# Delta rule attention on one core: key products in a spare bank, projections in another step, another order of masks and copies

## The chip, the core and the metric

The kernel runs on one core of a Trainium2 chip. The metric is the time of one launch on the device in microseconds (us), lower is better. Engines are named as in the profile: PE is TensorE's matmuls and PEld its weight loads, DVE is VectorE, ACT is ScalarE, POOL is GpSimd, SP is SyncE, which only issues DMAs here.

## What is computed

A four-layer network; every layer is a modulated layernorm, an attention block, another layernorm and a feed-forward block. The change touches the attention of layer 0, a gated delta rule over 4 sequences of 512 tokens with 16 key heads and 2 value heads for each:

```
mixed = silu(causal_conv4(x @ w_qkv)); z = x @ w_z          # q, k: 16 heads, v: 32 heads, 128 wide
for t in tokens:                                             # per value head, state Sm is 128 x 128
    Sm = Sm * exp(g[t])
    Sm = Sm + outer(k[t], (v[t] - k[t] @ Sm) * beta[t])
    o[t] = q[t] @ Sm
out = (rmsnorm(o * silu(z)) * norm_w) @ w_out
```

## The kernel before

The token loop is worked in chunks of 128 tokens. For each key head (a round, `q`) there are four stages, `a` = 0 to 3, one for each chunk; the 64 stages of the 16 key heads run as one software pipeline, written out for four rounds and looped four times (`nc.Fori`). In a stage `t`, for both value heads `j` and all four sequences at once:

- steps `i` = 0 to 5 build the inverse of a triangular 128x128 matrix for the chunk in hand by repeated squaring. Each step is: `turn_power` (PE transposes), `power` (ACT, four half copies for one head, out of the transposes' bank), `square_power` (PE, 4 products), then `power_c` (ACT) and `grow` (DVE, an addition) on what came out. The next step's transposes wait for `power_c`. This is one chain through PE, ACT and PE for the whole stage.
- between these pieces PE runs the recurrence of the chunk before (`v_turn`, `ks`, `z_prod`, `w_prod`, `x_prod`, `qs`, `pu`, `ku`, `y_turn`, `w_out`), and the projections of the next key head: items 0 to 7 are values (stage a=0), 8 to 11 keys (a=1), 12 to 15 queries (a=2). One item is `project` (PE, 4 matmuls of 512 columns), `tap` (ACT), `convolve` (DVE, three instructions), `silu` (ACT). Items from 8 on all use the one bank `PJ_A`, so each waits until the one before is convolved. `project_z` and `turn_kq` use `PJ_B`.
- at the end of the stage the key and query products of the next chunk are made: `kk_prod` into `PJ_A`, `qk_prod` into `PJ_B`; DVE masks them (`kk_mask`, `qk_mask`), makes the decay matrix of each head with a scan (`decay`), and multiplies the two into the next stage's starting matrix (`start_power`, which sets `v_u`, for which the next stage's first `turn_power` waits). `inverse` finishes the triangular inverse, `collect` adds `w_out`'s result, out of banks `B_AUX` (7) and 5, to the residual `x_res`; the next stage's first `v_turn` writes `B_AUX` and waits for it.

Every engine's order is written out by hand: `tensor_stage` (PE), `scalar_stage` (ACT), `vector_stage` (DVE), `pool_stage` (POOL), each a plain list in program order. An engine that waits holds back all behind it. `after(engine, semaphore, n)` is a wait that is left out when n is not positive. In step 4 before, PE runs

```
kk_prod(pe, t)
square_power(pe, t, i, 0)
qk_prod(pe, t)
square_power(pe, t, i, 1)
for j in HEADS: y_turn(pe, t, j)
```

`y_turn` transposes the normalised output into banks 5 and 6, ACT's `y_copy` brings it to `ww`, and `w_out` multiplies it with the output weights in step 5. `mean_sq` is ACT's sum of squares of the output (four pairs of instructions for one head), POOL's `rms` makes the factor `rho` of it, and DVE's `normed` applies it.

Of the kernel before, what the change touches and what calls it, by code (L numbers as in the profile page):

```python
# [465 lines left out]
def delta_pipeline(k, ph, gates, rates):  # L466
# [99 lines left out]
    def project(pe, q, n):  # L566
        N = count(q, n)
        if n == 0:
            after(pe, s["v_kk"], NC * q)
            after(pe, s["vz_in"], 32 * q)  # L570
        if n == V_ITEMS:
            after(pe, s["v_kk"], NC * q + 1)
            after(pe, s["kq_in"], 32 * q)
        if n == V_ITEMS + K_ITEMS:
            after(pe, s["v_kk"], NC * q + 2)
        if n == 1:
            after(pe, s["v_qk"], NC * q)
        if 1 < n < V_ITEMS:
            pe.wait_ge(s["v_cv"], N - 1)
        if n > V_ITEMS:  # L580
            pe.wait_ge(s["v_cv"], N)
# [6 lines left out]
    def project_z(pe, q, m):  # L588
        t = NC * q + (1, 1, 1, 1, 2, 2, 3, 3)[m]
        if m == 0:  # L590
            after(pe, s["v_qk"], t)
        if m == 2 or m == 4:
            pe.wait_ge(s["v_qk"], t + 1)
        if m % 2 or m == 6:
            pe.wait_ge(s["a_z"], 2 * NC * q + m)
# [18 lines left out]
    def kk_prod(pe, t):  # L614
        q, a = t // NC, t % NC
        if t < 0:
            pe.wait_ge(s["v_cv"], K_ITEMS + Q_ITEMS)
        elif a < NC - 1:
            pe.wait_ge(s["v_cv"], count(q, (V_ITEMS - 1, V_ITEMS + K_ITEMS, ITEMS)[a]))
        else:  # L620
            pe.wait_ge(s["v_kk"], t)
        par, c = next_par(t), next_chunk(t)
        each(pe, PJ_A, lambda b: key(par, c, b), lambda b: key(par, c, b)).then_inc(s["t_kk"], 1)

    def qk_prod(pe, t):
        q, a = t // NC, t % NC
        if t < 0:
            pe.wait_ge(s["a_sq"], 2 * NC)
        elif a == 0:
            pe.wait_ge(s["v_cv"], count(q, V_ITEMS))  # L630
        elif a == 1:
            pe.wait_ge(s["a_z"], 2 * NC * q + 2)
        else:
            pe.wait_ge(s["a_sq"], turned(q, NC if a == 2 else 2 * NC))
        par, c = next_par(t), next_chunk(t)
        each(pe, PJ_B, lambda b: key(par, c, b), lambda b: query(par, c, b)).then_inc(s["t_qk"], 1)
# [90 lines left out]
    def w_out(pe, t, j):  # L727
        h, c = hs[j], rec_chunk(t)
        pe.wait_ge(h["a_yt"], t + 1)
        if c == 0:  # L730
            pe.wait_ge(s["p_wb"], t // NC + 1)
        for b in range(NB):
# [6 lines left out]
    def tensor_stage(pe, t):  # L739
        q, a = t // NC, t % NC  # L740
        old = rec_chunk(t) > 0
        for i in range(6):
# [29 lines left out]
            if i == 2:  # L772
# [5 lines left out]
                if a == 2: turn_kq(pe, q, 1)  # L778
# [4 lines left out]
                if a == 2: project(pe, q, 14)  # L783
# [1949 lines left out]
```

## Time and profile before

| | us |
|---|---|
| median of 3 runs | 6501.39 |
| the runs | 6496.47, 6501.39, 6502.17 |
| the profiled execution, its own time | 6495.86 |
| its span, first to last instruction | 6494.1 |
| the delta rule's stretch of it | about 190 to 3320 |

The profile is of one execution, and lies just under the three timed runs. Busy times are of the whole span; a row of the timeline has its start, its length from the first start to the last end of the merged instructions, engine and line, output and inputs, and in brackets how long the engine had been idle and what ended that. L585 is `project`, L558 any group of 8 products of a recurrence step (its operands tell which), L563 transposes, L646 `turn_power`, L660 `square_power`, L733 `w_out`, L827 `tap`, L870 `power`, L876 `power_c`, L832 `silu`, L895 `mean_sq`, L903 `y_copy`, L1004 `convolve`, L1056 `decay`, L1066 `start_power`, L1083 `inverse`, L1149 `collect`, L1231 POOL's `injected`.

### The profile page before, as it was taken

How to read it: one execution, taken by the hardware profiler on the slowest of the kernel's cores; microseconds unless marked ns; L12 is line 12 of the kernel's file. 1: busy time of each engine (PE TensorE's matmuls, PEld its weight loads, DVE VectorE, ACT ScalarE, POOL GpSimd, SP SyncE). 2: the span in 40 equal slices, each digit the busy share in tenths (PEclk: the TensorE clock that was granted, in tenths of full speed). 3: DMA queues.
4: the chain of work that ended last, by engine and by line, in shares of the span. 5: the costliest groups of instructions: out<-in, count | busy, mean ns of one | idle time of the engine just before them, and what ended most of it. 6: DMA issues, size and time to landing. Idle time of an engine off the chain costs nothing. (4 is left out here: it accounts for less than half of the span.)

```text
span 6494.1 us, 91678 instructions
## 1 busy us (share of the span) xinstructions
PE 5343.2 (82%) x30758; PEld 3962.9 (61%) x30798; DVE 3718.8 (57%) x7849; ACT 3137.3 (48%) x9493; POOL 1141.8 (18%) x1216
## 2 busy tenths in 40 slices
PE   4889989999899998999979997888867773577769
PEld 2678777778777777877765555555444442343335
DVE  3666666666666666667653334555335555666661
ACT  1566666666566666666641113444225554333321
POOL 1222222222222222222210001111000000222210
PEclk7999999999999999999989998999978986788879
DMA  1000000000000000000010001000000000000000
GB/s 37 14 21 17 17 16 17 16 19 19 18 16 17 16 17 21 17 16 17 16 44 1 1 10 57 1 1 1 16 19 1 1 1 8 17 1 0 0 20 13
DMA packets 47176, 93.40 MB, mean 14 GB/s; under 512 B 11984, under 2 KB 19184, under 8 KB 45712
## 3 DMA queue, kind: packets, MB, share of 16 engines
q1 hardware_dynamic: 46736, 88.07, 4.3%
q8 instruction: 211, 3.46, 0.2%
q14 instruction: 229, 1.88, 0.1%
HBM read 85.67 MB, written 2.38 MB: 14 GB/s over the span
## 5 line engine op out<-in xcount | busy, mean ns | idle before, releaser
L870 ACT ACTIVATE dh_pb<-bank 64x128 f32<-64x128 f32 x3072 | 831.2, 271 | 253.7 <-PE bank L646 218.9
L660 PE MATMUL bank<-dh_cw,dh_pb 128*128 128x128 f32 x5120 | 692.0, 278 | 118.4 <-ACT dh_pb L870 118.1
L660 PEld LDWEIGHTS bank<-dh_cw,dh_pb 128*128 128x128 f32 x5120 | 634.0, 192 | 191.3 <-ACT dh_pb L870 156.9
L1004 DVE SCALAR_TENSOR_TENSOR dh_kq<-bank,dh_conv_kq,dh_kq 128x511 f32<-128x511 f32 (+2 forms) x408 | 305.5, 749 | 165.1 <-ACT dh_kq L827 152.6
L876 ACT ACTIVATE dh_cw<-bank 128x256 f32<-128x256 f32 x640 | 246.6, 385 | 282.1 <-PE bank L660 274.9
L1004 DVE SCALAR_TENSOR_TENSOR dh_v<-bank,dh_conv_v,dh_v 128x511 f32<-128x511 f32 (+2 forms) x384 | 284.2, 747 | 91.3 <-ACT dh_v L827 82.2
L585 PE MATMUL bank<-hT,dh_w_kq 128*128 128x512 f32 x544 | 273.0, 626 | 58.8 <-DVE dh_kq L1004 51.9
L1679 PE MATMUL bank<-moe_h_split,moe_w 128*128 x1160 | 273.8, 383 | 24.9 <-PEq L88 15.4
L1940 POOL TENSOR_TENSOR blk_att_e<-blk_att_e,blk_att_block_share 128x128 f32<-128x128 f32 (+3 forms) x256 | 185.0, 723 | 476.1 <-DVE blk_att_block_share L1913 476.1
L598 PE MATMUL bank<-dh_w_vz,hT 128*128 128x256 f32 x1024 | 245.5, 383 | 22.0 <-ACT dh_zs L838 22.0
L1075 DVE TENSOR_TENSOR dh_cw<-dh_cw,bank 128x256 f32<-128x256 f32 x512 | 210.4, 411 | 82.8 <-ACT dh_cw L876 82.8
L1098 DVE TENSOR_TENSOR dh_zz<-dh_zz,bank 128x512 f32<-128x512 f32 x130 | 89.3, 687 | 283.0 <-PE bank L558 281.1
L1518 ACT ACTIVATE moe_mlp_silu<-bank 128x512 f32<-128x512 f32 x100 | 59.7, 597 | 394.1 <-PE bank L1685 394.1
L585 PE MATMUL bank<-hT,dh_w_vz 128*128 128x512 f32 x512 | 242.5, 596 | 8.6 <-DVE dh_v L1004 8.6
L1532 DVE TENSOR_TENSOR moe_mlp_prod<-moe_mlp_silu,bank 128x512 f32<-128x512 f32 x100 | 68.8, 688 | 315.7 <-ACT moe_mlp_silu L1518 315.7
L262 POOL TENSOR_TENSOR ln_rstd<-ln_var_eps,nhalf 128x16 f32<-128x16 f32 x8 | 23.2, 2902 | 1264.8 <-DVE ln_var_eps L252 1264.8
L1239 POOL TENSOR_TENSOR dh_ntoff<-dh_kkm,dh_et 64x256 f32<-64x256 f32 x128 | 91.9, 722 | 847.2 <-PE bank L558 847.2
L1839 PE MATMUL bank<-ident,blk_att_e 128*128 128x128 f32 x640 | 130.6, 315 | 131.6 <-POOL blk_att_e L1940 125.8
L733 PE MATMUL bank<-dh_wo_gated,dh_ww 128*128 128x256 f32 x1040 | 236.1, 380 | 0.0
L1829 PE MATMUL bank<-blk_km,blk_q 128*128 128x128 f32 (+3 forms) x512 | 215.9, 538 | 21.0 <-PEq L88 21.0
L598 PEld LDWEIGHTS bank<-dh_w_vz,hT 128*128 128x128 f32 x1024 | 184.5, 190 | 54.6 <-ACT dh_zs L838 34.8
L646 PE MATMUL bank<-ident,dh_cw 128*128 128x128 f32 x1280 | 203.8, 276 | 14.9 <-ACT dh_cw L876 14.9
(399 smaller groups left out, 13143.0 us busy)
## 6 DMA issues: line engine op xcount, KB each, us to landing
dh_rates<-delta_rates SPq DMA_DIRECT2D x130, 256.0 KB, 3.2
dh_w_vz<-in_L_wvz SPq DMA_DIRECT2D x17, 512.0 KB, 3.2
mod_w<-in_L_wmod SPq DMA_DIRECT2D x4, 1536.0 KB, 6.3
dh_w_kq<-in_L_wkq SPq DMA_DIRECT2D x18, 256.0 KB, 2.6
dh_wo<-in_L_wo SPq DMA_DIRECT2D x16, 256.0 KB, 3.7
moe_w<-in_L_w13T SPq DMA_DIRECT2D x1, 3200.0 KB, 16.1
x_res<-in_x SPq DMA_DIRECT2D x1, 2048.0 KB, 8.2
mla_wA<-in_L_wA SPq DMA_DIRECT2D x1, 2048.0 KB, 8.8
```

What stands on the lines that cost most here:

```text
L585: last = pe.matmul(pj_bank(n), w[:, kk, :], k.hT[:, kk, n % NB, :], start=(kk == 0), stop=(kk == KD - 1))
L598: last = pe.matmul(bank[PJ_B][:, i * D:(i + 1) * D], k.hT[:, kk, 2 * (m % 2) + i, m // 2 * P:(m // 2 + 1) * P], wvz[:, kk, RPH * DH:], sta ...
L646: last = pe.transpose(bank[TURN][:, (2 * j + g) * P:(2 * j + g + 1) * P], src[:, 0, 2 * g:2 * g + 2, :].rearrange("p b n -> p (b n)"), k.i ...
L660: last = pe.matmul(square(j)[:, b, :, :], pb[j][:, b, :], src[:, :, b, :], start=True, stop=True)
L733: last = pe.matmul(bank[OUT[b // 2]][:, (b % 2) * D:(b % 2 + 1) * D], ww[j][:, b, :], wob[:, j, b, :], start=(j == 0 and b % 2 == 0), stop ...
L870: last = act.activation(out[half, :, o, half], src[halves[o], :, half], ACT.Copy)
L876: act.activation(cw[j][:, 0, :, :], square(j)[:, :, 0, :], ACT.Copy).then_inc(h["a_c"], 1)
L1004: dve.scalar_tensor_tensor(y, pj_bank(n)[:, 0:S - i], taps(n)[:, TAPS - 1 - i:TAPS - i], y, ALU.mult, ALU.add).then_inc(s["v_cs" if i < TA ...
L1075: dve.tensor_tensor(cw[j][:, 1, :, :], old[:, 1, :, :], square(j)[:, :, 1, :], ALU.add).then_inc(h["v_c"], 1)
L1679: last = pe.matmul(bank[:, :], w13[:, kk, which, m * P:(m + 1) * P], seq(hs[:, j, :, :, :], b)[:, kk, :], start=(n == 0), stop=(n == 3 * K ...
L1829: pe.matmul(bank[t][:, 0:keys(t)], qT(head)[:, t * P:(t + 1) * P], kT(head)[:, 0:keys(t)], start=True, stop=False, skip_group_check=True)
L1940: pool.tensor_tensor(ev, ev, row_bc(bc[:, 1, n % 2, 0:keys(t) // BLOCK], BLOCK), ALU.mult)\
```

## The change

- `kk_prod` and `qk_prod` both go to `B_AUX`, the bank that `qs` and `v_turn` use earlier in the stage and `w_out` after it. `kk_prod` waits for the last reader of that bank (DVE's `q_state` of head 1, or ACT's `v_scaled`) and no longer for a convolution; `qk_prod` waits for `kk_mask`; `w_out` of head 0 waits for `qk_mask`. `project` and `project_z` wait for the last users of their banks, which are no longer the masks.
- Step 4 on PE becomes `kk_prod`, `square_power` 0, `square_power` 1, `qk_prod`; `y_turn` goes to step 5, behind `turn_power`. On ACT `y_copy` goes between the two `power` groups of step 5.
- On DVE the end of the stage becomes `kk_mask`, `normed` x2, `grow` x2, `qk_mask`, `decay` x2, `start_power` x2 (before: `normed` x2, `decay` 0, `grow` 0, `kk_mask`, `grow` 1, `decay` 1, `qk_mask`, `start_power` x2).
- In stage a=1 `project` 10 moves from step 3 to the end of step 2, and `project` 11 from behind `ku` 1 to ahead of the step's first `square_power`. In a=2 `project` 14 and 15 each move forward and change places with `turn_kq` 1 and 2. Taps, convolutions, squares and norms of these items follow on ACT and DVE.

```
@@ -566,19 +566,16 @@
...
         if n == 0:
-            after(pe, s["v_kk"], NC * q)
+            after(pe, s["v_cv"], N)
             after(pe, s["vz_in"], 32 * q)
+        elif n == 1:
+            after(pe, s["a_sq"], 2 * NC * q)
+        elif n <= V_ITEMS:
+            after(pe, s["v_cv"], N - 1)
+        else:
+            pe.wait_ge(s["v_cv"], N)
         if n == V_ITEMS:
-            after(pe, s["v_kk"], NC * q + 1)
             after(pe, s["kq_in"], 32 * q)
-        if n == V_ITEMS + K_ITEMS:
-            after(pe, s["v_kk"], NC * q + 2)
-        if n == 1:
-            after(pe, s["v_qk"], NC * q)
-        if 1 < n < V_ITEMS:
-            pe.wait_ge(s["v_cv"], N - 1)
-        if n > V_ITEMS:
-            pe.wait_ge(s["v_cv"], N)
         w = wvz[:, :, n // NB * DH:(n // NB + 1) * DH] if n < V_ITEMS else \
...
@@ -586,12 +583,11 @@
...
     def project_z(pe, q, m):
-        t = NC * q + (1, 1, 1, 1, 2, 2, 3, 3)[m]
         if m == 0:
-            after(pe, s["v_qk"], t)
-        if m == 2 or m == 4:
-            pe.wait_ge(s["v_qk"], t + 1)
-        if m % 2 or m == 6:
+            pe.wait_ge(s["v_cv"], count(q, V_ITEMS))
+        elif m == 4:
+            pe.wait_ge(s["a_sq"], turned(q, NC))
+        else:
             pe.wait_ge(s["a_z"], 2 * NC * q + m)
...
@@ -612,28 +608,17 @@
...
     def kk_prod(pe, t):
-        q, a = t // NC, t % NC
-        if t < 0:
-            pe.wait_ge(s["v_cv"], K_ITEMS + Q_ITEMS)
-        elif a < NC - 1:
-            pe.wait_ge(s["v_cv"], count(q, (V_ITEMS - 1, V_ITEMS + K_ITEMS, ITEMS)[a]))
-        else:
-            pe.wait_ge(s["v_kk"], t)
+        if t >= 0 and rec_chunk(t):
+            pe.wait_ge(hs[1]["v_qs"], carried(t))
+        elif t >= 0:
+            pe.wait_ge(hs[1]["a_vs"], t + 1)
         par, c = next_par(t), next_chunk(t)
-        each(pe, PJ_A, lambda b: key(par, c, b), lambda b: key(par, c, b)).then_inc(s["t_kk"], 1)
+        each(pe, B_AUX, lambda b: key(par, c, b), lambda b: key(par, c, b)).then_inc(s["t_kk"], 1)
 
     def qk_prod(pe, t):
-        q, a = t // NC, t % NC
-        if t < 0:
-            pe.wait_ge(s["a_sq"], 2 * NC)
-        elif a == 0:
-            pe.wait_ge(s["v_cv"], count(q, V_ITEMS))
-        elif a == 1:
-            pe.wait_ge(s["a_z"], 2 * NC * q + 2)
-        else:
-            pe.wait_ge(s["a_sq"], turned(q, NC if a == 2 else 2 * NC))
+        pe.wait_ge(s["v_kk"], order(t) + 1)
         par, c = next_par(t), next_chunk(t)
-        each(pe, PJ_B, lambda b: key(par, c, b), lambda b: query(par, c, b)).then_inc(s["t_qk"], 1)
+        each(pe, B_AUX, lambda b: key(par, c, b), lambda b: query(par, c, b)).then_inc(s["t_qk"], 1)
 
...
@@ -724,11 +709,13 @@
...
 
-    def w_out(pe, t, j):
+    def w_out(pe, t, j, more=True):
         h, c = hs[j], rec_chunk(t)
...
             pe.wait_ge(s["p_wb"], t // NC + 1)
+        if j == 0:
+            after(pe, s["v_qk"], t + 1 if more else 0)
         for b in range(NB):
...
@@ -775,23 +762,23 @@
...
                 if a == 1: project(pe, q, 9)
-                if a == 2: turn_kq(pe, q, 1)
+                if a == 2: project(pe, q, 14)
                 if old: qs(pe, t, 1)
...
                 if a == 0: project(pe, q, 5)
-                if a == 2: project(pe, q, 14)
+                if a == 1: project(pe, q, 10)
+                if a == 2: turn_kq(pe, q, 1)
                 if a == 3: turn_kq(pe, q, 5)
...
                 if a == 0: project(pe, q, 6)
-                if a == 1: project(pe, q, 10)
-                if a == 2: turn_kq(pe, q, 2)
+                if a == 1: project(pe, q, 11)
+                if a == 2: project(pe, q, 15)
                 square_power(pe, t, i, 0)
...
                 if a == 0: project(pe, q, 7)
-                if a == 1: project(pe, q, 11)
-                if a == 2: project(pe, q, 15)
+                if a == 2: turn_kq(pe, q, 2)
                 if a == 3: turn_kq(pe, q, 6)
...
@@ -799,10 +786,10 @@
...
                 square_power(pe, t, i, 0)
+                square_power(pe, t, i, 1)
                 qk_prod(pe, t)
-                square_power(pe, t, i, 1)
+            if i == 5:
                 for j in HEADS: y_turn(pe, t, j)
-            if i == 5:
                 square_power(pe, t, i, 0)
...
@@ -917,7 +904,12 @@
...
                 continue
-            for j in HEADS: power(act, t, i, j)
+            if i == 5:
+                power(act, t, i, 0)
+                for j in HEADS: y_copy(act, t, j)
+                power(act, t, i, 1)
+            else:
+                for j in HEADS: power(act, t, i, j)
             if i == 1:
...
@@ -947,10 +939,11 @@
...
                     silu(act, q, 13)
-                    squares(act, q, 1)
+                    tap(act, q, 14)
                 power_c(act, t, 3, 1)
                 if a == 0: tap(act, q, 5)
-                if a == 2: tap(act, q, 14)
+                if a == 1: tap(act, q, 10)
+                if a == 2: squares(act, q, 1)
                 if a == 3: squares(act, q, 5)
...
@@ -958,17 +951,16 @@
...
                     silu(act, q, 9)
-                    tap(act, q, 10)
-                if a == 2: squares(act, q, 2)
+                    tap(act, q, 11)
+                if a == 2:
+                    silu(act, q, 14)
+                    tap(act, q, 15)
                 mean_sq(act, t, 0)
...
                     tap(act, q, 7)
-                if a == 1: tap(act, q, 11)
-                if a == 2:
-                    silu(act, q, 14)
-                    tap(act, q, 15)
+                if a == 2: squares(act, q, 2)
                 if a == 3: squares(act, q, 6)
...
@@ -983,7 +975,6 @@
...
                 for j in HEADS: power_c(act, t, 5, j)
-                for j in HEADS: y_copy(act, t, j)
             if i == 5:
...
@@ -1040,12 +1031,12 @@
...
         for j in HEADS: after(dve, hs[j]["p_nt"], t + 1)
-        dve.tensor_tensor(kkm[:, :, :], b4(PJ_A), mask_bc(k.neglt[:, :], NB), ALU.mult).then_inc(s["v_kk"], 1)
+        dve.tensor_tensor(kkm[:, :, :], b4(B_AUX), mask_bc(k.neglt[:, :], NB), ALU.mult).then_inc(s["v_kk"], 1)
 
...
         for j in HEADS: after(dve, hs[j]["p_pt"], t + 1)
-        dve.tensor_tensor(qkm[:, :, :], b4(PJ_B), mask_bc(k.le[:, :], NB), ALU.mult).then_inc(s["v_qk"], 1)
+        dve.tensor_tensor(qkm[:, :, :], b4(B_AUX), mask_bc(k.le[:, :], NB), ALU.mult).then_inc(s["v_qk"], 1)
 
...
@@ -1179,23 +1170,23 @@
...
         if a == 1: convolve(dve, q, 9)
-        if a == 2: norms(dve, q, 1)
+        if a == 2: convolve(dve, q, 14)
         if old: q_state(dve, t, 1)
...
         if a == 1: convolve(dve, q, 10)
-        if a == 2: convolve(dve, q, 14)
+        if a == 2: norms(dve, q, 1)
         if a == 3: norms(dve, q, 5)
         if a: state(dve, t, 0)
-        if a == 2: norms(dve, q, 2)
+        if a == 1: convolve(dve, q, 11)
+        if a == 2: convolve(dve, q, 15)
         grow(dve, t, 4, 0)
...
         if a: state(dve, t, 1)
-        if a == 1: convolve(dve, q, 11)
-        if a == 2: convolve(dve, q, 15)
+        if a == 2: norms(dve, q, 2)
         if a == 3: norms(dve, q, 6)
...
@@ -1204,13 +1195,11 @@
...
             query_vectors(dve, q)
+        kk_mask(dve, t)
         for j in HEADS: normed(dve, t, j)
-        decay(dve, t, 0)
-        grow(dve, t, 5, 0)
-        kk_mask(dve, t)
-        grow(dve, t, 5, 1)
-        decay(dve, t, 1)
+        for j in HEADS: grow(dve, t, 5, j)
         qk_mask(dve, t)
+        for j in HEADS: decay(dve, t, j)
         for j in HEADS: start_power(dve, t, j)
...
@@ -1440,8 +1429,9 @@
...
             for j in HEADS: v_turn(pe, 0, j)
-            for f in (ks, z_prod, w_prod, x_prod, qs, pu, y_turn, w_out):
+            for f in (ks, z_prod, w_prod, x_prod, qs, pu, y_turn):
                 for j in HEADS: f(pe, 0, j)
+            for j in HEADS: w_out(pe, 0, j, more=False)
 
...
```

## Rows read from the trace of the kernel before

**Rows 1.** Busy time by stretch: length, engines' busy us, granted clock, DMA.
```profile
190.00:3320.00 3130.00, 2843.65 (x19678) 2442.95 (x19676) 2061.73 (x3572) 2007.65 (x6442) 775.94 (x800) 1.00 0.06 17
```

**Rows 2.** Waits between 500 and 3200 us: total, times, longest.
```profile
PE bank L660 <- ACT dh_pb L870: 107.8, 124, 1.3
...
PE bank L558 <- DVE dh_kq L1004: 39.1, 27, 1.6
```

**Rows 3.** Timeline, the end of a stage a=0, PE and ACT.
```profile
1015.55 1.16 PE L558 MATMUL bank<-dh_kq 128*128 128x128 f32 x8 [0.88 <-DVE dh_v L1004]
1015.76 2.27 ACT L870 ACTIVATE dh_pb<-bank 64x128 f32<-64x128 f32 x8
...
1016.93 1.16 PE L660 MATMUL bank<-dh_cw,dh_pb 128*128 128x128 f32 x8 [0.22 <-ACT dh_pb L870]
...
1020.59 0.60 PE L646 MATMUL bank<-ident,dh_cw 128*128 128x128 f32 x4
...
1022.49 1.16 PE L660 MATMUL bank<-dh_cw,dh_pb 128*128 128x128 f32 x8 [1.30 <-ACT dh_pb L870]
```

**Rows 4.** Timeline, steps 2 to 4 of the stage a=1 behind it.
```profile
1051.03 1.06 PE L660 MATMUL bank<-dh_cw,dh_pb 128*128 128x128 f32 x8
1051.06 2.32 DVE L1004 SCALAR_TENSOR_TENSOR dh_kq<-bank,dh_conv_kq,dh_kq 128x511 f32<-128x511 f32 x3 [1.87 <-ACT dh_kq L827]
...
1051.92 0.38 PE L646 MATMUL bank<-ident,dh_cw 128*128 128x128 f32 x2
...
1052.56 0.44 PE L646 MATMUL bank<-ident,dh_cw 128*128 128x128 f32 x2 [0.26 <-ACT dh_cw L876]
...
1053.03 2.27 ACT L870 ACTIVATE dh_pb<-bank 64x128 f32<-64x128 f32 x8 [0.53 <-PE bank L646]
...
1059.07 1.98 PE L585 MATMUL bank<-hT,dh_w_kq 128*128 128x512 f32 x4 [1.68 <-DVE dh_kq L1004]
...
1060.89 1.05 PE L660 MATMUL bank<-dh_cw,dh_pb 128*128 128x128 f32 x8
...
1061.09 0.69 ACT L827 ACTIVATE dh_kq<-bank,dh_conv_kq 128x512 f32<-128x512 f32 x1 [3.00 <-PE bank L585]
...
1061.98 0.38 ACT L876 ACTIVATE dh_cw<-bank 128x256 f32<-128x256 f32 x1 [0.20 <-PE bank L660]
1062.26 0.30 ACT L895 ACTIVATE dh_zz<-dh_yy 128x128 f32<-128x128 f32 x1
...
1063.43 0.62 ACT L832 ACTIVATE dh_kq<-dh_kq 128x512 f32<-128x512 f32 x1
...
1063.95 2.26 ACT L870 ACTIVATE dh_pb<-bank 64x128 f32<-64x128 f32 x8
```

**Rows 5.** Timeline, the same two points of the stage a=2 behind it.
```profile
1113.90 2.26 ACT L870 ACTIVATE dh_pb<-bank 64x128 f32<-64x128 f32 x8
...
1120.86 1.16 PE L660 MATMUL bank<-dh_cw,dh_pb 128*128 128x128 f32 x8 [1.30 <-ACT dh_pb L870]
```

**Rows 6.** Timeline, ends of two stages a=3; the first ends a loop pass.
```profile
965.07 1.73 DVE L1066 TENSOR_TENSOR dh_c<-dh_kkm,dh_et 64x256 f32<-64x256 f32 x4
...
1163.96 1.21 DVE L1056 TENSOR_TENSOR_SCAN dh_et<-dh_rates,dh_inj 128x512 f32<-128x512 f32 x1
...
1166.02 1.04 POOL L1231 TENSOR_TENSOR dh_inj<-ident,dh_R 128x512 f32<-128x512 f32 x1
1166.34 1.80 DVE L1056 TENSOR_TENSOR_SCAN dh_et<-dh_rates,dh_inj 128x512 f32<-128x512 f32 x1
...
1167.13 1.16 PE L660 MATMUL bank<-dh_cw,dh_pb 128*128 128x128 f32 x8 [1.30 <-ACT dh_pb L870]
...
1168.64 2.21 DVE L1066 TENSOR_TENSOR dh_c<-dh_kkm,dh_et 64x256 f32<-64x256 f32 x4
...
1170.88 0.85 DVE L1083 TENSOR_TENSOR dh_ttb<-dh_cw,bank 64x256 f32<-64x256 f32 x2
...
1171.78 1.28 DVE L1149 TENSOR_TENSOR x_res<-x_res,bank 128x512 f32<-128x512 f32 x2
```

## Prediction, made before the changed kernel ran

> **What bounds the kernel now.** I read the page's slices first, for where PE is full, then the busy time by stretch, which places the delta rule between 190 and 3320 us, and there PE is busy 2844 of 3130 us at a granted clock of 1.00, while DVE and ACT stand at some 2000 each [rows 1]. So PE is the bound of this stretch, its clock has nothing more to give, and what a change can take away is the 286 us in which PE stands, 18 us for each of the 16 rounds. The list of waits, PE's rows alone, says what those are: mostly `square_power` waiting for ACT's half copies (108 us in some 14 rounds), then the key products waiting for a convolution (39 us, two of a round's three such places) [rows 2]. The timeline of one round shows where they lie. The reader is to see two kinds. In step 5 of every stage PE has issued the transposes at 1020.59 and stands until 1022.49, since ACT's copies must come between; this 1.30 us of waiting is there in a=2 and a=3 too, and as long in a=1 [rows 3, 5, 6]. Ahead of `kk_prod` PE stands 0.88 us in a=0 [rows 3], and likewise in a=1 and a=2, until the last projection is convolved and `PJ_A` is free (39.1 us over 27 of them, 1.45 each [rows 2]).
>
> **A frame for the sum.** Call P the start of ACT's `power` group of step 4 and T the start of step 5's first `square_power`. P is set by ACT (its sums of squares and silu stand ahead of it), T ends the short chain behind it. Before, T lies behind P by 22.49 - 15.76 = 6.73 us in a=0 [rows 3], as much in a=1 and a=3, and by 6.96 in a=2 [rows 5]. From T to the next stage's first transposes the PE list is unchanged, so a gain in T is handed on whole, unless DVE's tail is late.
>
> **Step 4 and 5, all stages.** What is left of P to T in the new order: the first squaring starts 1.17 behind P (15.76 to 16.93) [rows 3]. The second needs the second half of eight copies, 2.27 us of them [rows 3], so it starts at P + 2.30, after 0.24 us of waiting. A group of 8 products takes PE 0.89 (1051.03 to 1051.92 [rows 4]), so `qk_prod` starts at P + 3.19 and the transposes at P + 4.08. From them to the copies is 0.64 (0.60 of transposes, and 0.03 of hand-over: 1052.56 + 0.44 to 1053.03 [rows 4]), and 1.17 more to the squaring: T = P + 5.89. The two `y_turn`, 0.87, now run inside these 1.81 us, so about 0.5 of the 1.30 us stall is left. Gain: 6.73 - 5.89 = 0.84, in a=2 1.07. The new waits cost nothing on these paths. `qk_prod` wants `kk_mask`, which DVE has done near P + 2.8 in a=0 and earlier elsewhere; if it came after P + 3.19, all of it would be paid. `w_out` at T + 0.89 wants `qk_mask`, done near T - 0.9. `kk_prod`'s own wait, for a reader of bank 7 in step 2, is long over. `y_copy` between the two `power` groups delays only the second group, which is wanted 4.3 us behind T's transposes. `y_turn` wants `normed` and gets it 0.2 to 1 us early; `normed` hangs on POOL's factor, not on the new order. Ahead of the loop and after it the same waits are once only, under 2 us either way; I take 0.
>
> **Projections in a=0: nothing moves,** P stays. The wait of `kk_prod` (0.88) is gone, but PE then waits for ACT's copies at P + 1.17 all the same: it is worth nothing by itself. Stage gain 0.84.
>
> **Projections in a=1: a loss.** The items share one bank, so each waits for the convolution before it. Item 9 is convolved at 1051.06 + 2.32 = 1053.38 [rows 4]. Before, PE did `turn_power` and `ku` 0 first. Now `project` 10 stands at 1051.92, where the transposes began [rows 4], and waits 1.5 us to 1053.42. Its tap begins 2.02 after it (59.07 to 61.09), the convolution 0.72 after that and lasts 2.32 (61.09 to 61.81) [rows 4]: convolved at 1058.48. `project` 11 now comes ahead of the squarings of step 3; PE reaches it at 1056.57 (1053.42, 1.82 for a projection as 1059.07 to 1060.89, 0.44 of transposes, 0.89) and waits to 1058.53, 1.96 us. Behind it are still its own 1.82 us, a squaring, `ku` 1 and a squaring: the last starts at 1062.13, where it was 1060.89 [rows 4]. From there ACT's chain is `power_c` after 1.09 (60.89 to 61.98), 0.28 on the sums of squares, 1.17 for them (62.26 to 63.43), 0.52 for a silu, then P [rows 4]: 1062.13 + 3.06 = 1065.19 against 1063.95. P is 1.24 late, T = 1071.08 against 1070.67. Stage: 0.41 us lost. The two old waits (1.68 [rows 4], and that ahead of `kk_prod`) have become 1.50 and 1.96 earlier ones, and the work that used to fill time ahead of them now comes behind them. The bounds of this term: if ACT had slack there, P would stay and 0.84 be gained; if both new waits were paid on top of the old path, 3.46 - 0.84 = 2.6 us would be lost. I take the chain's figure, as every link of it has a row.
>
> **Projections in a=2.** `project` 14 goes ahead of `turn_kq` 1, 3.4 us earlier, behind a convolution that ends just there (0.2 us of wait, in place of a like one). `turn_kq` 2 and 3 are later, so the squares of them are; I find ACT's copies P at 1114.20 against 1113.90 [rows 5], T at 1120.09 against 1120.86. Gain 0.77. Two ACT instructions more or less ahead of P move this by 0.5 at most either way.
>
> **DVE's tail.** Both scans now stand behind `qk_mask` (near T - 1.6 in a=3), then `start_power`, `inverse` 0, `collect`. POOL's `injected` follows each scan, so it now runs beside the second scan and beside `start_power`. A scan alone takes 1.21, beside it 1.80 [rows 6]; `start_power` 1.73 alone, 2.21 beside it [rows 6]. In a=1 and a=2 two `project_z` follow and hide the tail; in a=0 POOL is held elsewhere and the tail ends in time. In a=3 the scans start at T - 1.0, `start_power` ends at T + 4.1, in time for the transposes at T + 5.34, `inverse` at T + 4.95 where `w_out` is done at T + 4.65 (71.78 - 67.13) [rows 6]. So `collect` starts 0.3 late, and `v_turn` with it: of 0.84 0.56 is left. In the last a=3 of each of four loop passes POOL is idle and 0.84 stays. Bounds: 0 added, or each of POOL's two 1.04 us paid in full, 1.0 us more than I take: 12 stages, 12 us. By the Trainium skill (SBUF — State Buffer, "SBUF: two separate sides") the port pair of VectorE and GpSimd is an exclusive lock for a whole instruction; the trace leans that way, as the scan that began 0.72 us before POOL's end lost 0.59. With the lock paid in full by DVE the sum would be 18 us instead of 30.
>
> **Sum.** 16 x (0.84 - 0.41 + 0.77) = 19.2; a=3: 12 x 0.56 + 4 x 0.84 = 10.1; together 29.3 us. Of the profiled execution's 6495.9 this leaves 6466.6. The median of the runs lies 5.5 above that execution, so the forecast is 6472, a gain of 0.45%.
>
> **Rivals.**
> (1) *No change that can be told, within 0.2% (13 us)*: the step-5 gap is filled, but a=1 loses its 2.6 in full (35 us more over 16 rounds than I take) or the tail costs its upper bound with half of that. For it: the new order puts two bank waits ahead of work that used to cover them. Against: each link is chained from rows. 6472 + 35 = 6507 at most for the first; with the tail at its bound and half of it, 6502.
> (2) *Slower*: head-of-line blocking on ACT in a=1. `tap` 10 now stands ahead of step 3's `power` groups, and `tap` 11 ahead of the sums of squares of head 0; ACT holds all copies of the repeated squaring until each projection is through. If each such hold delayed the squaring by a whole bank cycle (2.02 + 0.72 + 2.32 = 5.06 us from project to project [rows 4]) instead of letting it proceed, a=1 would lose 5.06 more, 81 us in all: 6553. It decides once a=1 loses 2.6 us more than I take (13 + 29 over 16). Against it: `tap` 10 ends at 1056.0, 0.1 us behind the transposes whose copies it holds.
> (3) *More than I say*: P moves earlier, since `kk_prod` no longer ends a chain of convolutions and ACT is less crowded; with 0.84 in every stage and a=1 too, 64 x 0.84 = 54 us, 6448.
>
> **How the numbers follow.** What a measurement of this kernel can tell from no change is about 0.2%, 13 us: the three runs span 6. Chances: forecast 0.66, (1) 0.14, (2) 0.12, (3) 0.08. Faster by over 0.2% is the forecast and (3), 0.74; within, 0.14; slower 0.12. The range runs from two thirds of the way to (3) to the forecast plus the tail's 12 and half a us more in a=1: 6455 to 6492. That leaves out somewhat less than 2 in 10.
>
> **What would show it.** Right: `kk_prod` no longer waits for DVE in any stage; PE's wait in step 5 falls from 1.30 to near 0.5; P to T is near 5.9 everywhere; in a=1 there are waits of near 1.5 and 2.0 ahead of `project` 10 and 11, and its P lies later; `v_turn` of a=0 waits for `collect` longer than before, except after a loop pass. Wrong: a wait of `qk_prod` for `kk_mask`, of `w_out` for `qk_mask` or of the first transposes for `start_power`; or a second scan over 2 us.

## The result and the profile after

The changed kernel takes 6488.43 us (median of 16 runs, 6481.94 to 6493.3), the kernel before 6498.82 (16 runs, 6494.57 to 6504.95): a ratio of 0.9984, 95% interval 0.9977 to 0.999. So it gained 10.4 us, by the interval 6.5 to 15, where 29.3 were forecast. The time lies inside the range and the sign is right, but the gain of 0.16% is less than the 0.2% (13 us) that the prediction took as the least that can be told from no change. The forecast of a gain over 0.2% did not come true.

The busy time by stretch and the list of waits of the changed kernel answer to [rows 1, 2]:

```profile
190.00:3320.00 3130.00, 2865.47 (x19716) 2460.89 (x19716) 2109.55 (x3584) 2008.21 (x6449) 830.34 (x800) 0.99 0.06 17
```

```profile
PE bank L645 <- ACT dh_pb L857: 102.0, 152, 1.4
PE bank L582 <- DVE dh_kq L995: 44.8, 41, 1.8
...
PE bank L563 <- DVE x_res L1140: 9.0, 11, 0.8
```

The kernel before has one more row of this kind, its `project` behind a convolution:

```profile
PE bank L585 <- DVE dh_kq L1004: 24.3, 26, 1.7
```

Four things are to be seen. The key products' wait for a convolution (39.1 us) is gone from the list. `project`'s wait for one has grown from 24.3 us in 26 places, two a round, to 44.8 us in 41, three a round: half of what went away came back there. And `v_turn`'s wait for `collect` is new among PE's rows. The squarings (now L645) wait for ACT almost as long as before, 102 us against 107.8, but in 152 pieces and not in 124.

The lines have moved: L645 is `square_power`, L631 `turn_power`, L582 `project`, L720 `w_out`, L857 `power`, L995 `convolve`, L1066 `grow`, L1047 `decay`, L1057 `start_power`, L1074 `inverse`, L1140 `collect`, L1220 POOL's `injected`. (`x8` of a group counts the instructions of PE in the trace, two for each of the code's four products.) The timeline of a stage a=0, PE, answers to [rows 3]:

```profile
1014.83 2.40 PE L645 MATMUL bank<-dh_cw,dh_pb 128*128 128x128 f32 x16 [1.36 <-ACT dh_pb L857]
1017.07 1.06 PE L558 MATMUL bank<-dh_kq 128*128 128x128 f32 x8
1017.96 0.60 PE L631 MATMUL bank<-ident,dh_cw 128*128 128x128 f32 x4
1018.40 1.04 PE L563 MATMUL bank<-ident,dh_yy 128*128 128x128 f32 x8
1019.77 1.16 PE L645 MATMUL bank<-dh_cw,dh_pb 128*128 128x128 f32 x8 [0.34 <-ACT dh_pb L857]
1020.77 1.46 PE L720 MATMUL bank<-dh_wo_gated,dh_ww 128*128 128x256 f32 x6
```

The same stretch, PE's weight loads, shows where the second of the two squarings really begins:

```profile
1014.83 0.97 PEld L645 LDWEIGHTS bank<-dh_cw,dh_pb 128*128 128x128 f32 x8 [1.55 <-ACT dh_pb L857]
1016.07 0.97 PEld L645 LDWEIGHTS bank<-dh_cw,dh_pb 128*128 128x128 f32 x8 [0.27 <-ACT dh_pb L857]
1016.96 0.97 PEld L558 LDWEIGHTS bank<-dh_kq 128*128 128x128 f32 x8
```

And ACT's, with P of this stage:

```profile
1013.66 2.27 ACT L857 ACTIVATE dh_pb<-bank 64x128 f32<-64x128 f32 x8
```

As in the prediction, P is the start of ACT's `power` group of step 4 and T the start of step 5's first `square_power`. The wait in step 5 fell from 1.30 to 0.34 us, `y_turn` fills the rest, and T lies 6.11 us behind P, where 6.73 were before and 5.89 forecast.

To compare kernels I take the time from the start of `w_out` in one stage to the next (T plus 1.00 in every stage). Apart from the stages with a low clock, told below, and the ends of the loop's passes, the numbers repeat within 0.02 us over all rounds. Worked out so, in us, each stage ahead of the arrow to the one behind it, and what that is per round against before:

| kernel | a0→a1 | a1→a2 | a2→a3 | a3→a0 | per round |
|---|---|---|---|---|---|
| before | 48.18 | 50.19 | 46.27 | 49.69 | |
| after | 48.72 | 49.51 | 45.56 | 49.84 | -0.70 |
| the forecast | 48.59 | 49.42 | 45.43 | 49.13 | -1.76 |
| e1, `y_turn` only | 47.67 | 49.69 | 45.77 | 49.66 | -1.54 |
| e10, banks only | 48.41 | 50.28 | 46.51 | 50.03 | +0.90 |
| e2, both of these, items as before | 47.44 | 49.31 | 45.55 | 49.83 | -2.20 |
| e9, items only | 49.43 | 50.21 | 46.26 | 49.68 | +1.25 |
| e4, banks and items | 49.67 | 50.46 | 46.51 | 50.02 | +2.33 |
| e3, after with late injection | 48.73 | 49.51 | 45.56 | 49.07 | -1.46 |
| e7, e2 with late injection | 47.47 | 49.34 | 45.56 | 49.07 | -2.89 |
| e8, e7 with `project_z` early | 47.48 | 47.03 | 42.88 | 49.08 | -7.86 |

### The profile page after: what moved, and what is told of

Its sections match the earlier page's. It is cut to its first block and busy times, and to the rows that moved or that the text cites. A ratio compares the mean times of both kernels' runs of the same rounds, so it can differ in the third digit from the quotient of the medians.

```text
span 6482.1 us, 91750 instructions
## 1 busy us (share of the span) xinstructions
PE 5360.2 (83%) x30798; PEld 3975.0 (61%) x30798; DVE 3759.5 (58%) x7849; ACT 3136.4 (48%) x9493; POOL 1195.5 (18%) x1216
## 5 line engine op out<-in xcount | busy, mean ns | idle before, releaser
L857 ACT ACTIVATE dh_pb<-bank 64x128 f32<-64x128 f32 x3072 | 831.3, 271 | 272.0 <-PE bank L631 238.7
L645 PE MATMUL bank<-dh_cw,dh_pb 128*128 128x128 f32 x5120 | 701.6, 281 | 112.9 <-ACT dh_pb L857 111.4
L645 PEld LDWEIGHTS bank<-dh_cw,dh_pb 128*128 128x128 f32 x5120 | 635.7, 193 | 191.0 <-ACT dh_pb L857 164.3
L995 DVE SCALAR_TENSOR_TENSOR dh_kq<-bank,dh_conv_kq,dh_kq 128x511 f32<-128x511 f32 (+2 forms) x408 | 305.3, 748 | 184.0 <-ACT dh_kq L814 172.8
L582 PE MATMUL bank<-hT,dh_w_kq 128*128 128x512 f32 x544 | 276.3, 632 | 82.6 <-DVE dh_kq L995 75.2
L995 DVE SCALAR_TENSOR_TENSOR dh_v<-bank,dh_conv_v,dh_v 128x511 f32<-128x511 f32 (+2 forms) x384 | 284.0, 747 | 91.3 <-ACT dh_v L814 82.3
L582 PE MATMUL bank<-hT,dh_w_vz 128*128 128x512 f32 x512 | 242.5, 596 | 8.5 <-DVE dh_v L995 8.5
L1066 DVE TENSOR_TENSOR dh_cw<-dh_cw,bank 128x256 f32<-128x256 f32 x512 | 206.6, 412 | 73.4 <-ACT dh_cw L863 73.4
L720 PE MATMUL bank<-dh_wo_gated,dh_ww 128*128 128x256 f32 x1040 | 237.0, 381 | 0.0
L1236 POOL TENSOR_TENSOR dh_pto<-dh_qkm,dh_et 128x512 f32<-128x512 f32 x128 | 163.2, 1275 | 285.2 <-PE bank L558 285.2
```

Of the source, the lines that this page charges most:

```text
L582: last = pe.matmul(pj_bank(n), w[:, kk, :], k.hT[:, kk, n % NB, :], start=(kk == 0), stop=(kk == KD - 1))
L645: last = pe.matmul(square(j)[:, b, :, :], pb[j][:, b, :], src[:, :, b, :], start=True, stop=True)
L720: last = pe.matmul(bank[OUT[b // 2]][:, (b % 2) * D:(b % 2 + 1) * D], ww[j][:, b, :], wob[:, j, b, :], start=(j == 0 and b % 2 == 0), stop ...
L857: last = act.activation(out[half, :, o, half], src[halves[o], :, half], ACT.Copy)
L995: dve.scalar_tensor_tensor(y, pj_bank(n)[:, 0:S - i], taps(n)[:, TAPS - 1 - i:TAPS - i], y, ALU.mult, ALU.add).then_inc(s["v_cs" if i < TA ...
L1066: dve.tensor_tensor(cw[j][:, 1, :, :], old[:, 1, :, :], square(j)[:, :, 1, :], ALU.add).then_inc(h["v_c"], 1)
```

## The experiments

Kernels of one group ran on one chip beside the kernel before: 6499.66 us for e1 to e4, 6497.17 for e7 to e9, 6500.0 for e10 and the two repeats.

**e1, `y_turn` alone.** The kernel before, with

```diff
                 square_power(pe, t, i, 1)
-                for j in HEADS: y_turn(pe, t, j)
             if i == 5:
+                for j in HEADS: y_turn(pe, t, j)
                 square_power(pe, t, i, 0)
```

and `y_copy` between the `power` groups, as in the change.

> The kernel before with one edit: y_turn behind step 5's transposes and y_copy between ACT's two power groups. Sizes theory (the change's gain is this edit, cut short by small costs of the rest): here the squaring of step 4 that waits, the key product, the second squaring and the query product alternate, so T lies 1.17 + 1.00 + 0.89 + 0.89 + 1.81 = 5.76 us behind P instead of 6.73. Three of a round's four stages are 0.9 to 1.0 us shorter; the end of a=3 is set by DVE's unchanged tail and keeps its place. 2.9 us a round, 16 rounds: 46 us less than before, near 6453, well below the whole change. Rival (the gain came from the key products leaving PJ_A and PJ_B, or from the new mask order): this edit alone gives at most what the whole change gave, 10 us, near 6488 or the old time, because y_turn then waits for the normalised output.

Measured: 6475.77 us, ratio 0.9963 (0.9948 to 0.9977). This is 24 us less than before, over twice the gain of the whole change and half of the 46 that I expected. PE's timeline of a stage a=0 shows what was missed:

```profile
1014.72 1.06 PE L660 MATMUL bank<-dh_cw,dh_pb 128*128 128x128 f32 x8
1015.61 0.39 PE L646 MATMUL bank<-ident,dh_cw 128*128 128x128 f32 x2
1016.25 0.44 PE L646 MATMUL bank<-ident,dh_cw 128*128 128x128 f32 x2 [0.25 <-ACT dh_cw L876]
1016.52 1.04 PE L563 MATMUL bank<-ident,dh_yy 128*128 128x128 f32 x8
1017.89 1.16 PE L660 MATMUL bank<-dh_cw,dh_pb 128*128 128x128 f32 x8 [0.34 <-ACT dh_pb L870]
```

With the second squaring right ahead of the transposes, those of head 1 wait for `power_c` of it: the four transposes span 0.91 us (1015.61 to 1016.52) and not 0.44. T is 2.28 us behind their start, where it was 1.90 before [rows 3] and 1.81 in my sum. The other part of the sum, the transposes 3.95 behind P, holds in the trace. In a3→a0 the gain is 0.03 only, as expected: DVE's tail is unchanged there.

**e2, without the moved projections.** The changed kernel with items 10, 11, 14, 15 and the turns 1 and 2 in the order of before, on all three engines, as:

```diff
-                if a == 1: project(pe, q, 10)
-                if a == 2: turn_kq(pe, q, 1)
+                if a == 2: project(pe, q, 14)
                 if a == 3: turn_kq(pe, q, 5)
             if i == 3:
                 if a: ku(pe, t, 0)
                 if a == 0: project(pe, q, 6)
-                if a == 1: project(pe, q, 11)
-                if a == 2: project(pe, q, 15)
+                if a == 1: project(pe, q, 10)
+                if a == 2: turn_kq(pe, q, 2)
```

> The changed kernel with projections 10, 11, 14, 15, turn_kq 1 and 2 and all that follows them on ACT and DVE in the order of before. Sizes theory: P of a=1 comes back by 1.24 us, the wait ahead of kk_prod stays away, a=2 gains 0.2 to 0.3: 1.3 us a round, some 20 us below the changed kernel, near 6467. Rival (with the key products out of the way the earlier projections help, or cost nothing): the same time as the changed kernel or slower, 6488 or more.

Measured: 6467.05 us, 0.9948 (0.9931 to 0.9964). The table has it where it was expected: a0→a1 1.28 us shorter than in the changed kernel, a1→a2 0.20, the rest equal.

**e3, POOL's injection later.** The changed kernel with

```diff
-        for j in HEADS: injected(pool, t, j)
         if a == 3: value_scale(pool, q)
         for j in HEADS: off_diagonal(pool, t, j)
+        for j in HEADS: injected(pool, t, j)
```

> The changed kernel with POOL's injected behind off_diagonal in each stage, so that it no longer stands beside DVE's start_power. Contention theory: start_power's four instructions fall from 3.26 to 1.73 us, collect of a=3 starts when w_out is done, v_turn of a=0 comes 0.77 us earlier in 12 of 16 rounds: 9 us less than the changed kernel, near 6479. Rival (the tail is long because both scans stand behind qk_mask, whatever POOL does): no change beyond 2 us.

Measured: 6480.57 us, 0.997 (0.9959 to 0.9982); a3→a0 is 0.77 shorter, all else equal. The end of a stage a=3 in the changed kernel, DVE and then POOL and PE, answers to [rows 6]:

```profile
1162.55 2.33 DVE L1047 TENSOR_TENSOR_SCAN dh_et<-dh_rates,dh_inj 128x512 f32<-128x512 f32 x2
1164.80 3.26 DVE L1057 TENSOR_TENSOR dh_c<-dh_kkm,dh_et 64x256 f32<-64x256 f32 x4
...
1168.97 1.28 DVE L1140 TENSOR_TENSOR x_res<-x_res,bank 128x512 f32<-128x512 f32 x2
...
1163.90 2.99 POOL L1220 TENSOR_TENSOR dh_inj<-ident,dh_R 128x512 f32<-128x512 f32 x2
...
1163.55 1.16 PE L645 MATMUL bank<-dh_cw,dh_pb 128*128 128x128 f32 x8 [0.34 <-ACT dh_pb L857]
...
1170.31 0.66 PE L563 MATMUL bank<-ident,dh_v 128*128 128x128 f32 x4 [0.82 <-DVE x_res L1140]
```

The same in e3, DVE:

```profile
1159.30 2.33 DVE L1047 TENSOR_TENSOR_SCAN dh_et<-dh_rates,dh_inj 128x512 f32<-128x512 f32 x2
1161.54 1.71 DVE L1057 TENSOR_TENSOR dh_c<-dh_kkm,dh_et 64x256 f32<-64x256 f32 x4
1163.28 0.85 DVE L1074 TENSOR_TENSOR dh_ttb<-dh_cw,bank 64x256 f32<-64x256 f32 x2
1164.95 1.28 DVE L1140 TENSOR_TENSOR x_res<-x_res,bank 128x512 f32<-128x512 f32 x2 [0.82 <-PE bank L720]
```

`start_power` takes 1.71 us and not 3.26, and `collect` waits for `w_out` alone and no longer stands behind `start_power` and `inverse`. The rival, that the order of the scans makes the tail long whatever POOL does, is out.

**e4, `y_turn` back in step 4.** The changed kernel with the edit of e1 undone.

> The changed kernel with y_turn back at the end of step 4 and y_copy back ahead of step 5's copies; banks, items and mask order as changed. Sizes theory: T lies 6.9 to 7.0 us behind P in every stage instead of 6.0, of which the end of a=3 gives 0.8 back since the tail then has time: 2.8 us a round, 45 us above the changed kernel, near 6533, and 35 above the kernel before. Rival (the spare bank and the free projections are themselves a gain): between the changed kernel and the one before, 6488 to 6499.

Measured: 6540.35 us, 1.0066 (1.005 to 1.0083). Without `y_turn` in step 5 the rest of the change is a loss of 2.33 us a round. The rival, that the spare bank and the moved projections are a gain by themselves, is out.

**e9, the moved projections alone,** on the kernel before: the edits to `tensor_stage`, `scalar_stage` and `vector_stage` that e2 takes out.

> The kernel before with one part of the change: projections 10, 11, 14 and 15, with their taps, silus and convolutions, at the earlier places of the change and turns 1 and 2 later; the key products stay in the projections' bank and y_turn in step 4. My theory says that this part loses 1.28 us in a=1 and 0.20 in a=2, as taking it out of the changed kernel gained, less what kk_prod's wait for the convolution (0.88 in a=1) gives back since projection 11 is convolved earlier: slower than before by 0.6 to 1.5 us a round, 10 to 24 us, so 6510 to 6524. Rival: the earlier items are bought back in full by kk_prod's shorter waits in a=1 and a=2, and the move is a loss only beside the bank change: within 5 us of before, 6495 to 6505.

Measured: 6530.21 us, 1.0053 (1.0036 to 1.0069); 6 us above the top of what was expected. The time per round was as expected (1.25, so 20 of the 33 us), five stages with a low clock of 1.6 us each came on top in the profiled execution, and some 5 us are not accounted for. PE's timeline of a=1:

```profile
1059.14 1.98 PE L585 MATMUL bank<-hT,dh_w_kq 128*128 128x512 f32 x4 [1.35 <-DVE dh_kq L1004]
...
1064.25 1.98 PE L585 MATMUL bank<-hT,dh_w_kq 128*128 128x512 f32 x4 [1.80 <-DVE dh_kq L1004]
...
1069.67 1.06 PE L558 MATMUL bank<-dh_kq 128*128 128x128 f32 x8
```

In the kernel before the same `kk_prod` stands behind a wait:

```profile
1064.18 1.16 PE L558 MATMUL bank<-dh_kq 128*128 128x128 f32 x8 [1.32 <-DVE dh_kq L1004]
```

In a=1 that wait is 1.32 us; the 0.88 in my expectation is the one of a=0. In e9 `kk_prod` (1069.67) has lost it though it still uses `PJ_A`, and nothing came of it: T stays 6.71 us behind P (6.72 before). The rival, that shorter waits there would pay for the move, is out. In a=2 the move costs 0.02 us.

**e10, banks and order alone.** The changed kernel with the projections of e2 and `y_turn` and `y_copy` in step 4 as in e4.

> The kernel before with the key products in the spare bank, both squarings of step 4 ahead of qk_prod, and the change's order of masks and copies on DVE, but y_turn and y_copy in step 4 and the projections in the order of before. With the runs so far this closes a square: y_turn alone took 0.51 us off three stages, both without the projections took 0.70 to 0.87 off them. My theory: without something to do between the transposes and the squaring of step 5, the second squaring of step 4 coming directly ahead of the transposes makes PE wait longer in step 5, and y_turn in step 4 stands in front of the transposes: the parts are worth 0.4 us more together than one by one, so this kernel is within 1 us a round of before, on the slow side: +0.85 a round by subtracting (the run with y_turn put back, +3.03 a round on the changed kernel, less 0.70 and 1.48), near 6512. Rival: each part's worth adds up by itself; both together gained 2.18 a round in all stages, y_turn 1.55 of it, so the banks alone gain 0.6 a round, near 6489.

Measured: 6516.55 us, 1.0025 (1.0015 to 1.0035); +0.90 us a round, by subtraction +0.85, and not -0.6. PE and ACT in a stage a=1:

```profile
1069.16 2.30 PE L645 MATMUL bank<-dh_cw,dh_pb 128*128 128x128 f32 x16 [1.35 <-ACT dh_pb L857]
1071.30 1.06 PE L558 MATMUL bank<-dh_kq 128*128 128x128 f32 x8
1072.19 1.04 PE L563 MATMUL bank<-ident,dh_yy 128*128 128x128 f32 x8
1073.07 0.60 PE L631 MATMUL bank<-ident,dh_cw 128*128 128x128 f32 x4
1074.97 1.16 PE L645 MATMUL bank<-dh_cw,dh_pb 128*128 128x128 f32 x8 [1.30 <-ACT dh_pb L857]
...
1068.00 2.25 ACT L857 ACTIVATE dh_pb<-bank 64x128 f32<-64x128 f32 x8
```

The transposes start 5.07 us behind P (1073.07 - 1068.00), where it was 4.83 before (20.59 - 15.76 [rows 3]), and T follows 1.90 behind them in both. So the new order costs 0.24 by itself in a=1 and a=3 (0.34 in a=0, 0.10 in a=2): the second squaring stands until the second half of the copies, while before `qk_prod` filled that time. What the order is good for is seen beside e1: with `qk_prod` ahead of the transposes, `power_c` of head 1 is done when they come. Before, T lies behind P by 4.83 + 1.90 = 6.73; in e1 3.95 + 2.28 = 6.23; in e10 5.07 + 1.90 = 6.97; with both, in a=0 of the changed kernel, 4.30 + 1.81 = 6.11. Moving `y_turn` is worth 1.54 us a round alone and 3.10 on top of the order (0.90 to -2.20).

**e7 and e8, towards a better kernel.** e7 is e2 and e3 in one. e8 is e7 and, with `silu_z` moved likewise on ACT,

```diff
                 kk_prod(pe, t)
+                if a == 1: project_z(pe, q, 2)
+                if a == 2: project_z(pe, q, 4)
                 square_power(pe, t, i, 0)
...
                 square_power(pe, t, i, 1)
-                if a == 1:
-                    project_z(pe, q, 2)
-                    project_z(pe, q, 3)
-                if a == 2:
-                    project_z(pe, q, 4)
-                    project_z(pe, q, 5)
+                if a == 1: project_z(pe, q, 3)
+                if a == 2: project_z(pe, q, 5)
```

> The changed kernel with two parts taken out together: projections 10, 11, 14, 15 and the turns 1, 2 in the order of before, and POOL's two injected products behind its off_diagonal, clear of DVE's start_power. My theory says the two losses lie in different stages (a=1 and a=2 for the projections, a=3 for the tail) and so add up: the step from e2 (6467) is the one that e3 showed in a=3, 0.77 us in 12 of the 16 rounds, 9 us, so near 6458, and v_turn of a=0 again about 6.0 us behind T. Rival: with the projections early, P of a=3 or the next stage's start is set by something else (ACT's copies or the output of the normed rows), and the tail is hidden anyway: within 2 us of e2, 6467.

> As e7, and in a=1 and a=2 the first of the two project_z at the end of step 5 goes to step 4, behind kk_prod, where PE stands 1.36 us for ACT's copies; its silu_z goes behind power_c 5 of head 1 on ACT. A project_z lasts some 2.6 us on PE, of which 1.36 would fill the wait, and the second one, which waited about 0.7 us for ACT's silu_z of the first, would no longer wait. If PE's waits are what a stage can still lose, each of the 32 stages a=1 and a=2 gains 1.3 to 2.0 us: 42 to 64 us, so 6395 to 6416. Rival: project_z reaches 1.2 us beyond the copies, and P to T is a chain of ACT and PE that ends the stage, so T comes 1.2 us later and ACT's silu_z (about 0.5) delays the copies of step 5 too; what the end of step 5 gives back is then covered by DVE's tail (start_power, collect, v_turn), which hangs on the squarings and not on project_z: a gain under 0.5 us a stage, above 6440, or a loss.

Measured: e7 6450.64 us, 0.993 (0.9913 to 0.9946), e8 6369.96 us, 0.9807 (0.979 to 0.9823). By the table the step from e2 to e7 is 0.76 in a3→a0, as expected, and 0.69 a round. The median fell by 16 us and not by 9: the profile of e7 has no stage with a low clock where e2's has three (about 4 us), and its chip was 2.5 us quicker on the kernel before. e8 gained 81 us more, above the 42 to 64. PE's timeline of a=2 in e7:

```profile
1104.64 2.30 PE L645 MATMUL bank<-dh_cw,dh_pb 128*128 128x128 f32 x16 [1.32 <-ACT dh_pb L857]
...
1114.92 1.89 PE L594 MATMUL bank<-dh_w_vz,hT 128*128 128x256 f32 x8
1117.50 1.99 PE L594 MATMUL bank<-dh_w_vz,hT 128*128 128x256 f32 x8 [0.69 <-ACT dh_zs L825]
1119.33 0.60 PE L631 MATMUL bank<-ident,dh_c 128*128 128x128 f32 x4
```

and in e8:

```profile
1077.78 1.99 PE L594 MATMUL bank<-dh_w_vz,hT 128*128 128x256 f32 x8 [0.31 <-ACT dh_ww L833]
1079.61 1.95 PE L645 MATMUL bank<-dh_cw,dh_pb 128*128 128x128 f32 x16
...
1084.10 1.16 PE L645 MATMUL bank<-dh_cw,dh_pb 128*128 128x128 f32 x8 [0.34 <-ACT dh_pb L855]
...
1089.44 1.89 PE L594 MATMUL bank<-dh_w_vz,hT 128*128 128x256 f32 x8
1091.17 0.60 PE L631 MATMUL bank<-ident,dh_c 128*128 128x128 f32 x4
```

The end of the stage got shorter by 2.68 us (4.41 from the first `project_z` to the transposes, now 1.73), and in the gap of step 4 the same work costs nothing in a=1 and 0.38 in a=2, where `project_z` first waits for its bank (0.31, ACT's `squares`) and the first squaring comes 1.77 behind P in place of 1.16. I had put a `project_z` at 2.6 us, by adding its wait to it; it takes 1.8, which hardly outlasts the gap. The rival, that T would come 1.2 us later and the gain stay under 0.5 a stage, is out: T is not moved in a=1 (6.01 behind P), and by 0.38 in a=2.

**The two kernels once more,** one execution each, for the stages with a low clock. In the changed kernel three of its segments are 1.3 us longer than in the other rounds. The busy time by stretch, around one of them:

```profile
811.00:812.00 1.00, 0.01 (x1) 0.01 (x1) 0.96 (x2) 0.94 (x5) 0.92 (x2) 1.00 0.00 0
812.00:813.00 1.00, 1.00 (x4) 1.00 (x5) 0.96 (x2) 0.96 (x4) 0.92 (x2) 0.51 0.00 0
...
814.00:815.00 1.00, 1.00 (x7) 1.00 (x6) 1.00 (x3) 0.64 (x2) 0.00 (x0) 0.50 0.00 0
815.00:816.00 1.00, 1.00 (x9) 1.00 (x9) 0.24 (x1) 0.29 (x1) 0.00 (x0) 0.78 0.00 0
```

> The changed kernel once more, one execution with a profile, to see the three stages of 1.3 us more whose TensorE clock fell to about a half for 2 to 3 us. If they belong to the kernel, they stand in the same rounds again; if they are an accident of the execution, they stand elsewhere or in another number. The other stages come out as in the first profile to 0.02 us either way.

> The kernel before once more, one execution with a profile, for the same question: its first profile had no such fall in the steady rounds. If the falls are an accident of the execution, one or more may stand here; if the kernel before is free of them, none.

Measured: 6489.37 and 6502.77 us. The changed kernel has three such stages again, but in rounds 2, 7 and 14 where they were in 3, 8 and 11; the kernel before again has none apart from the a=1 of its first round and the ends of the loop's passes, where PE is idle for some 6 us in both. So the place changes from execution to execution, while the number in the steady rounds, three and none, is the same in both profiles of either kernel; neither of my two answers is wholly right, and two profiles each are few. The profiles of e1, e2 and e3 have three each, e4 and e10 four, e9 five, e7 and e8 none. In all these profiles the falls lie in stages a=0 and a=1, at the first squaring of step 4. In 24 of the 25 of the changed kernel (both profiles), e2, e3, e4, e9 and e10, PE had stood for 1.36 us just ahead of it. In the other one, of e9, and in the three of e1 `kk_prod` stands inside the gap, between waits of 0.88 and 0.22; the kernel before has these same two waits in each a=0 and no fall behind them.

## Why the prediction was right in its sign and wrong in its size

**The frame and the chain hold.** P to T, what sets a stage, and a gain in T that is handed on whole: each segment of the table follows from them within the sizes below. `kk_prod` waits for no convolution, `qk_prod` and `w_out` for no mask, and the wait in step 5 fell to 0.34 us, which is 0.50 as the forecast counts it, from the last product's start plus its pitch (forecast: near 0.5).

**a=1, forecast -0.41, measured -0.54.** The two waits ahead of `project` 10 and 11 are there,

```profile
1050.70 1.98 PE L582 MATMUL bank<-hT,dh_w_kq 128*128 128x512 f32 x4 [1.34 <-DVE dh_kq L995]
...
1055.81 1.98 PE L582 MATMUL bank<-hT,dh_w_kq 128*128 128x512 f32 x4 [1.80 <-DVE dh_kq L995]
```

which is PE's timeline of the changed kernel; the waits of 1.50 and 1.96 that I gave are counted in the same way, and so 0.16 longer. e2 prices the move at 1.28 (P 1.24 late, as forecast) and e9 at 1.25 on the kernel before. The link-by-link chain was right, and it says that this part should have stayed out.

**P to T, the first mis-sized term: 5.89 forecast, 6.11 in a=0 and 6.01 to 6.02 in the other stages.** Two links failed. The first is "a group of 8 products takes PE 0.89", which I also used for the second squaring, a group that begins after a wait. `qk_prod` comes 1.00 behind its start (1016.07 to 1017.07), and so it is in every stage. The trace of before shows both sizes, since L660 at 1022.49 there was followed by `w_out` at 1023.49; I took the row of a group that had not waited. The rows of PE's weight loads show where the 0.11 lies: while PE runs, the first weight load of a group starts 0.11 ahead of its first product (1016.96 and 1017.07); behind a wait the two start together (1014.83).

The second is "so it starts at P + 2.30". That holds in a=1, a=2 and a=3 (2.31), but in a=0 it starts at P + 2.41 (1016.07 - 1013.66). By the code a squaring waits for ACT's copies and for DVE's `grow` of the step before, and I had reckoned with the copies alone. In a=0 this `grow` stands behind two convolutions and ends last, 1015.54 + 0.41 = 1015.95, where the copies end at 1015.93; in the other stages it is done before P + 0.1. DVE's timeline of this a=0:

```profile
1011.09 4.53 DVE L995 SCALAR_TENSOR_TENSOR dh_v<-bank,dh_conv_v,dh_v 128x511 f32<-128x511 f32 x6
1015.54 0.41 DVE L1066 TENSOR_TENSOR dh_cw<-dh_cw,bank 128x256 f32<-128x256 f32 x1
```

That `grow` is what holds the squaring in a=0 is read from these rows; no run moves it. The four stages together are 0.22 + 0.12 + 0.13 + 0.12 = 0.59 us a round, 9.4 us in all, of which the `grow` is less than 2.

**DVE's tail, the second: 0.28 us forecast, 0.77 measured.** `collect` starts at T + 5.42 where I had T + 4.95 and `v_turn` at T + 6.76 (1170.31 - 1163.55), before T + 5.99. The step that failed is "a scan alone takes 1.21, beside it 1.80; `start_power` 1.73 alone, 2.21 beside it": the scans began ahead of POOL and ran at 1.17 each, and both of POOL's products then stood beside `start_power`, which took 3.26. e3 takes POOL's part away and gets all 0.77 back. Against the 0.28 forecast that is 0.49 x 12 = 5.9 us. The Trainium skill (SBUF — State Buffer, "SBUF: two separate sides") has the port pair of VectorE and GpSimd as an exclusive lock that goes to whoever starts first. This trace agrees: the second scan, first by 0.2 us (1163.68, POOL 1163.90), kept its pace, while POOL's two products took 2.99 us for twice the 1.04 of [rows 6], and `start_power`, next on DVE, paid 1.55 (3.26 - 1.71). I had weighed the lock as a bound of 1.0 us beyond my figure and taken 0; half was due. (The 18 and 30 us of that passage are 17 and 29 by its own figures.)

**The clock, a term that I did not have.** Three stages with about 1.3 us more make 4.0 us; the kernel before has one such stage, the a=1 of its first round, of 1.6 us, which the changed kernel has not. So 2.4 us of the gain went there.

Together 9.4 + 5.9 + 2.4 = 17.7, which leaves 11.6 of the 29.3. The medians say 10.4 (6.5 to 15), and the two profiled executions, from which the terms are read, 11.9 (6495.86 - 6483.94). That it comes out so near is in part luck: the three ends of a loop pass alone differ among themselves by up to 1.1 us in one profile.

**The rivals.** (1), no change that can be told, is what came out by its bound of 0.2%, but not by its mechanism alone: the tail cost half of its upper bound, a=1 0.13 more and not 2.6, and the rest came from P to T and the clock, which no rival had. (2) did not happen: P of a=1 came 1.25 us late, as the chain said, and not 5 more. (3) was false where it lay: in a=1 P came later, not earlier. The larger gain was to be had in what the change left alone: its parts are worth -3.10 (`y_turn` on the new order), +0.90 (banks and order) and +1.50 (items) a round, and one part that it does not have, the gap in front of step 4's squaring, -4.97.

**What stays open.** What makes the clock fall after one of PE's 1.36 us waits and not after the same wait in the next round, or anywhere in the one profile of e7, which has that wait in a=0 and a=1 too. And whether the 0.11 us of a=0 goes away with `grow` ahead of the convolutions.

## What to carry to other kernels

Chain every moved piece link by link, even one that only "comes a bit earlier": in a pipeline where one bank makes items take turns, asking for the bank sooner moves its wait ahead of work that used to cover it. Look through all that an instruction waits for, not only the wait that ended last before: in a=0 `grow` ends last as soon as the squaring moves ahead of `qk_prod`. Removing a wait pays nothing where a second wait ends at the same time or later; put work into the gap (`y_turn`, `project_z`), taken from where the engine is the bound, and count a piece by its pitch without the wait in front of it. When a DVE operation is moved, ask which of POOL's will stand beside it there, and what it costs on DVE if POOL has started first.

## What the runs showed of the hardware

- A group of eight matmul instructions of 128 columns in float32, each with its weight load, takes PE 1.00 us to the next group if it began after a wait, 0.89 if not (after, a=0: 1016.07 to 1017.07; before, 1051.03 to 1051.92). The first weight load, 0.11 us ahead of its product, is covered only where PE was running before it. Two groups in a row take 1.78 without a wait (e8, 1079.61 to `qk_prod` at 1081.39), and 2.24 in a=0 of the changed kernel (1014.83 to 1017.07), where each of the two begins after one and 0.24 is the wait of the second.
- A fall of the granted clock from 1.00 to 0.50, the lower of its two levels, for some 3 us comes in 24 cases right behind a wait of PE of 1.36 us ahead of step 4's squaring; each fall costs 1.3 to 1.6 us. Not each such wait has one, and the waits of 1.30 us in step 5 of the kernel before had none in two profiles.
- Two of POOL's products of 128x512 made DVE's `start_power`, four products of 64x256, 3.26 us long where it takes 1.71 alone, while the scan that had begun before them kept its 1.2 us.
